# A fused attention and mixture-of-experts layer on one core: the key's rotation sum and the application of both layer norms, moved between VectorE and GpSimd

## The reference

```
xn  = (x - mean) / sqrt(var + 1e-5)                       # first layer norm
q   = rope(rms_norm(xn @ wq));  k = rope(rms_norm(xn @ wk));  v = xn @ wv      # 16 / 4 / 4 heads of 128
kc  = rms_norm(ctx @ wk_ctx);   vc = ctx @ wv_ctx
x1  = x + softmax(q @ [kc k]^T / sqrt(128) + causal) @ [vc v] @ wo
xn2 = (x1 - mean) / sqrt(var + 1e-5)                      # second layer norm
out = x1 + shared_ffn(xn2) + sum over the top 2 of 8 experts of weight * expert_ffn(xn2)
rope(k) = k * cos + rotate_half(k) * sin
```

## Time and profile before

| | |
|---|---|
| median of 3 runs | 366.74 us (364.2, 366.74, 368.2) |
| the profiled execution's own time | 366.01 us |
| its span | 364.3 us |
| mean granted clock of TensorE | 0.989 of full speed |
| instructions | 7426 |
| busy share of the span | PE 91%, PEld 61%, DVE 87%, ACT 72%, POOL 46% |

### The profile page before, as it was taken

One profiled execution on the slowest core, in us unless ns is written; L12 is line 12 of the kernel. 1 busy time (PEld: TensorE's weight loads), 2 busy tenths in 40 slices (PEclk: granted clock), 3 DMA queues, 4 the chain that ended last, 5 costly groups with the idle time before them and its releaser, 6 DMA issues.

```text
span 364.3 us, 7426 instructions
## 1 busy us (share of the span) xinstructions
PE 329.9 (91%) x2296; PEld 223.4 (61%) x2296; DVE 316.9 (87%) x602; ACT 263.7 (72%) x916; POOL 166.5 (46%) x241
## 2 busy tenths in 40 slices
PE   6788698799999999999999999999999999987894
PEld 6365455376667666866576657565856687754351
DVE  1779999998999899989999998999899987967643
ACT  3668989576986798679768976897599748447341
POOL 4467656652755175427532734263426230362600
PEclk9899989999999999999999999999999999999999
DMA  6977000000042005200300000000000000167844
GB/s 177 380 238 230 18 0 2 1 2 14 1 126 47 14 0 128 45 14 3 58 6 8 0 0 14 0 0 0 0 0 0 3 0 0 23 123 75 159 75 129
DMA packets 34835, 19.25 MB, mean 53 GB/s; under 512 B 24056, under 2 KB 32256, under 8 KB 34816
## 3 DMA queue, kind: packets, MB, share of 16 engines
q1 hardware_dynamic: 34816, 19.02, 20.6%
HBM read 12.20 MB, written 1.05 MB: 36 GB/s over the span
## 4 chain that ended last, share of the span: by engine, by line
PE 35%; DVE 24%; ACT 18%; issue 10%; POOL 6%; DMA 3%; SPq 1%; DVEq 1%; ACTq 0%; POOLq 0%
PE proj L1352 10%; ACT probs L549 7%; DVE probs L982 5%; PE pt_ps L1315 5%; PE turn L1261 3%; DVE nmax L970 3%; POOL q_rot L772 3%; PE o_ps L1325 3%; DVE pT_lo L908 3%; PE proj L1172 3%; PE sc_ps L1282 3%; ACT pT_hi L460 2%; DVE q_t L899 2%; ACT kc_junk L493 2%; DMA wq<-in_L_xattn_wq_dram 2%
## 5 line engine op out<-in xcount | busy, mean ns | idle before, releaser
L549 ACT ACTIVATE probs<-sc_ps,nbias,q_r 128x256 f32<-128x256 f32 x128 | 70.8, 573 | 2.8 <-DVE nbias L974 2.8
L772 POOL TENSOR_TENSOR q_rot<-q_t 128x512 f32<-128x512 f32 x32 | 42.4, 1325 | 41.3 <-DVE q_t L901 40.5
L982 DVE TENSOR_SCALAR probs<-probs,rden 128x256 f32<-128x256 f32 x128 | 51.2, 461 | 1.1
L460 ACT ACTIVATE pT_hi<-pt_ps 128x512 f16<-128x512 f32 x64 | 34.8, 597 | 10.1 <-PE pt_ps L1315 10.1
L493 ACT ACTIVATE q_junk<-proj 128x128 bf16<-128x128 f32 x128 | 34.0, 294 | 10.8 <-DVE q_t L901 10.8
L1172 PE MATMUL proj<-wq_hi,xT 128*128 128x512 f16 x128 | 39.2, 389 | 2.1 <-DVE wq_lo L892 2.1
L908 DVE SCALAR_TENSOR_TENSOR pT_lo<-pt_ps,pT_hi 128x512 f16<-128x512 f32 x64 | 40.9, 680 | 0.1
L970 DVE TENSOR_REDUCE nmax<-sc_ps 128x4 f32<-128x1024 f32 x32 | 38.8, 1214 | 1.5 <-PE sc_ps L1304 1.5
L729 POOL TENSOR_TENSOR q_r<-q_me,power 128x4 f32<-128x4 f32 x32 | 33.4, 1044 | 2.5
L460 ACT ACTIVATE qT_hi<-turn 128x512 f16<-128x512 f32 x32 | 19.5, 610 | 20.5 <-PE turn L1261 20.5
L1315 PE MATMUL pt_ps<-ident,probs 128*128 128x128 f32 x256 | 34.1, 277 | 0.2
(11 more groups left out here) (221 smaller groups left out, 882.8 us busy)
## 6 DMA issues: line engine op xcount, KB each, us to landing
wq<-in_L_xattn_wq_dram SPq DMA_DIRECT2D x4, 512.0 KB, 8.4
w<-in_L_ffn_w_dram SPq DMA_DIRECT2D x2, 1024.0 KB, 9.9
wq<-in_L_xattn_wo_dram SPq DMA_DIRECT2D x1, 2048.0 KB, 8.2
ctx_b<-in_ctx_dram SPq DMA_DIRECT2D x8, 128.0 KB, 2.0
out_dram<-x_all SPq DMA_DIRECT2D x4, 256.0 KB, 2.2
x_all<-in_x_dram SPq DMA_DIRECT2D x1, 896.0 KB, 12.0
wkc<-in_L_xattn_wk_ctx_dram SPq DMA_DIRECT2D x1, 512.0 KB, 3.9
wk<-in_L_xattn_wk_dram SPq DMA_DIRECT2D x1, 512.0 KB, 4.9
```

The lines of the kernel that those rows point to most:

```text
L460: return nc.scalar.activation(out_, in_, ACT.Copy, scale=scale)
L549: last = nc.scalar.activation(probs[:, h, :], sc_ps[:, h, :], ACT.Exp, bias=nbias[:, h:h + 1], scale=q_r[:, g, h:h + 1], accum_out=den[:, ...
L772: nc.gpsimd.tensor_tensor(q_rot[:], q_t1[:], q_t2[:], ALU.add).then_inc(q_added, 1)
L982: last = nc.vector.tensor_scalar(probs[:, h, :], probs[:, h, :], rden[:, h:h + 1], None, ALU.mult)
```

## The change

Three steps of rows change engine. `k_add` for the key of the next row goes from the end of DVE's g = 2 to POOL's g = 2, between `q_add` and `k_roots`. `ln_scale` for the next row goes from DVE's g = 1 to POOL's g = 0, right behind `ln_root`. `second_norm` for the row before goes from DVE's g = 2 to POOL's g = 1, right behind `l2_root`. In the prologue DVE still does `k_add(0)` and `ln_scale(0)`, and behind the rows it still does `second_norm(7)`; so each of the three moves in 7 of its 8 executions. DVE gains two waits in `scores_max` (for the first norm's application at g = 0, for the second's at g = 1), one in its own `second_norm` and one ahead of the last residual; they keep it from overwriting statistics that POOL still reads. On POOL the loop over rows 4 to 6 is written out.

```diff
--- before.py
+++ after.py
@@ -734,6 +734,12 @@
                 pool.wait_ge(ln_root1, nb + 1)
                 nc.gpsimd.tensor_tensor(ln_rs[:], ln_r1[:], scale_x[:], ALU.mult).then_inc(ln_rstd, 1)
 
+            def ln_scale(nb):
+                pool.wait_ge(ln_rstd, nb + 1)
+                seen(pool, ln_lo, nb)
+                nc.gpsimd.tensor_scalar(xs[:], x_all[:, nb, :], ln_mv[:, 0:1], ln_rs[:, 0:1],
+                                        ALU.subtract, ALU.mult).then_inc(ln_xs, 1)
+
             def ln_low(nb):
                 pool.wait_ge(ln_hi, nb + 1)
                 seen(pool, in_turned, nb)
@@ -743,6 +749,11 @@
                 seen(pool, l2_done, b)
                 rstd(ln2_mv, ln2_ve, ln2_rs, l2_aggr, l2_var, l2_rstd, b + 1)
 
+            def second_norm(b):
+                pool.wait_ge(l2_rstd, b + 1)
+                nc.gpsimd.tensor_scalar(xn2_all[:, b, :], x_all[:, b, :], ln2_mv[:, 0:1], ln2_rs[:, 0:1],
+                                        ALU.subtract, ALU.mult).then_inc(l2_done, 1)
+
             def kc_roots(nb):
                 seen(pool, kc_norm, nb)
                 inv_rms(kc_ss[:], kc_me[:], kc_r[:], eps_kc, kc_sq, kc_mean, kc_root, nb + 1)
@@ -750,6 +761,11 @@
             def k_roots(nb):
                 seen(pool, k_norm, nb)
                 inv_rms(k_ss[:], k_me[:], k_r[:], eps_k, k_sq, k_mean, k_root, nb + 1)
+
+            def k_add(nb):
+                pool.wait_ge(k_t12, nb + 1)
+                seen(pool, k_norm, nb)
+                nc.gpsimd.tensor_tensor(k_sum[:], k_t1[:], k_t2[:], ALU.add).then_inc(k_added, 1)
 
             def k_scale(nb):
                 pool.wait_ge(k_added, nb + 1)
@@ -800,6 +816,7 @@
                         q_add(*ahead_of(b, g, 2, last))
                     if g == 0 and first:
                         ln_root(b + 1)
+                        ln_scale(b + 1)
                     if g == 2 and not last:
                         kc_roots(b + 1)
                     if ahead_of(b, g, 2, last):
@@ -809,9 +826,12 @@
                             q_roots(*ahead_of(b, g, 2, last))
                     if g == 0 and not first and not last:
                         ln_root(b + 1)
+                        ln_scale(b + 1)
                     if g == 1 and not first:
                         l2_root(b - 1)
+                        second_norm(b - 1)
                     if g == 2 and not last:
+                        k_add(b + 1)
                         k_roots(b + 1)
                         k_scale(b + 1)
                         q_roots(b + 1, 0)
@@ -845,7 +865,7 @@
             row(1, False, False, cast_to(w1_b, w1_32, d_w1, w1_cast))
             row(2, False, False, cast_to(w3_b, w1_32, d_w3, w3_cast))
             row(3, False, False, cast_to(w2_b, w2_32, d_w2, w2_cast))
-            with pool.Fori(4, B - 1) as b:
+            for b in range(4, B - 1):
                 row(b, False, False)
             row(B - 1, False, True)
 
@@ -967,6 +987,10 @@
             def scores_max(b, g):
                 u = G * b + g
                 dve.wait_ge(s_done, u + 1)
+                if g == 0:
+                    dve.wait_ge(ln_xs, b + 1)
+                if g == 1:
+                    seen(dve, l2_done, b - 1)
                 nc.vector.tensor_reduce(nmax[:], sc_ps[:], AX_X, ALU.max, negate=True).then_inc(s_max, 1)
                 dve.wait_ge(s_max, u + 1)
                 dve.wait_ge(q_root, u + 1)
@@ -1000,6 +1024,7 @@
 
             def second_norm(b):
                 dve.wait_ge(l2_rstd, b + 1)
+                seen(dve, l2_done, b)
                 nc.vector.tensor_scalar(xn2_all[:, b, :], x_all[:, b, :], ln2_mv[:, 0:1], ln2_rs[:, 0:1],
                                         ALU.subtract, ALU.mult).then_inc(l2_done, 1)
 
@@ -1032,8 +1057,6 @@
             def row(b, first, last):
                 for g in range(G):
                     u = G * b + g
-                    if g == 1 and first:
-                        ln_scale(b + 1)
                     scores_max(b, g)
                     if g == 3 and first:
                         wo_split(0)
@@ -1041,12 +1064,8 @@
                         split_low(wv32[:], wv_hi[:], wv_lo[:], G + 2)
                     if ahead_of(b, g, 1, last):
                         q_low(*ahead_of(b, g, 1, last))
-                    if g == 1 and not first and not last:
-                        ln_scale(b + 1)
                     if g or not first:
                         p_low(u - 1)
-                    if g == 2 and not first:
-                        second_norm(b - 1)
                     if ahead_of(b, g, 2, last):
                         q_turn(*ahead_of(b, g, 2, last))
                     if g == 0 and not last:
@@ -1074,8 +1093,6 @@
                         v_low(b)
                     if g or not first:
                         o_low(u - 1, (g - 1) % G)
-                    if g == 2 and not last:
-                        k_add(b + 1)
                     if g == 0:
                         vc_low(b)
 
@@ -1139,6 +1156,7 @@
             o_low(G * B - 1, G - 1)
             e_scale(0)
             e_scale(1)
+            dve.wait_ge(l2_done, B - 1)
             residual(B - 1)
             e_scale(2)
             second_norm(B - 1)
```

## The result

The changed kernel takes **368.80 us** (median of 20 runs, 365.74 to 370.41) beside 366.48 us for the kernel before (20 runs): a ratio of **1.0057 [1.0034, 1.0081]**, or about 2.1 us. The forecast was 367.0 us and no measurable change: the range held, and the change is a little slower, by less than 1%. Its working did not hold everywhere. The six steady rows were forecast at +0.9 us and give +0.3; row 0 was forecast at -0.5 us and gives +1.3 in the profiled execution and, to judge by their longer times, more in most others.

The account below looks back on a forecast made before the run. PE, ACT and POOL in turn bound the steady rows, DVE in g = 0 alone. Rows 1 to 6 +0.9 and row 0 -0.5 gave +0.4: 366.4 us profiled, 367.1 against the median, stated 367.0; range 364.2 to 369.5 us.

Parts of the forecast that it names:

- the two terms of the sum: Whole kernel: rows 1 to 6 together +0.9 us and row 0 -0.5 us, giving +0.4 us.
- What bounds the kernel: Steady rows: PE last in g = 1, ACT, POOL, PE in g = 2, ACT in g = 3, DVE in g = 0 alone.
- DVE's busy time "about 13 us lower": Sign expected in the changed profile: DVE's busy time about 13 us lower, its waits for ACT in g = 3 longer.
- Rows 1 to 6, +0.15 us each: Steady rows: -0.06 second norm, +0.16 key's sum, +0.05 DVE's new waits; six rows make +0.9 us.
- the +0.16: POOL in g = 2, rows 1 to 6: the key's sum at 1.27 us starts the root 0.16 us late, whole into the row.
- The new wait at g = 0: DVE's added wait ahead of nmax in rows 1 to 6: 0 to +0.10 us per row, taken as +0.05.
- the second norm's gain: DVE in g = 2, rows 1 to 6: an earlier reciprocal lets POOL's first root come earlier, 0 to -0.06 us, taken as -0.06.
- The norms on POOL: POOL in g = 0 and g = 1: 0.67 us each, priced from x_lo, hidden in POOL's waits for ACT.
- Row 0, -0.5 us: Row 0: part of DVE's freed time counts and moves wo_lo forward; bounds -0.93 and 0 us, taken as -0.5.
- DVE as the bound: Rival, rows' DVE work: if all counted, 13.4 us gained and 353.4 us; only the key's sum, 359.0 us. Chance 0.11.
- The second: Rival, g = 2: a DVE instruction holds up POOL's key sum to 2.25 us; +6.8 us, 373.5 us. Chance 0.09.
- What the prediction held more likely there: g = 2 of steady rows: by the exclusive lock, k_add would hold up DVE's bias rather than be held.

Follow-up runs that it names:

- 3: 40 small TensorE products put in row 1's wait before the mix: changed kernel 366.96 us, ratio 1.0002; kernel before 366.09 us, 0.9992.
- 4: Changed kernel with DVE's second split of wo in row 0 in four pieces: 368.93 us, 1.0079; with 40 small TensorE products as well 367.31 us, 1.0009.
- 2: POOL's wo_lo in eight pieces: changed kernel 364.07 us, ratio 0.9930; kernel before 365.15 us, 0.9953.
- 6: POOL's scaling of wo and wo_lo each in eight pieces: changed kernel 364.41 us, ratio 0.9933; kernel before 364.13 us, 0.9926.

## Why the prediction was right, and where it was wrong

- **The range held, with some luck.** The time is 1.8 us above the forecast, and the two terms of the sum were off in opposite directions.
- **What bounds the kernel: right.** DVE lost 6.3 us of busy time and none of rows 1 to 6 got shorter. After the sum's place it waits for ACT in g = 2 and g = 3, as argued.
- **DVE's busy time "about 13 us lower": wrong, 6.3.** By groups, 13.4 us left DVE and the bias's group grew from 8.9 to 11.1 us, so the groups' sum fell by 10.9 (340.7 to 329.8). Records of neighbours overlap at their ends, the page counts the overlap once, and there was 4.6 us more of it before: I had read 13 us of groups as 13 us of engine.
- **Rows 1 to 6, +0.15 us each: right in sign, mis-sized.** Measured +0.04 between the two profiled executions, which is hardly more than their scatter: over all executions here the six rows take 213.12 to 213.29 us with the steps moved and 212.99 to 213.24 without. The key's sum cost 1.27 us as taken from q_rot, and k_me starts at its end. But of the +0.16 only +0.08 arrives: from ACT's squares of the context key (kc_junk) to the last reciprocal it is 10.07 us instead of 9.99. The new wait at g = 0 showed nothing, where 0.05 was taken; the second norm's gain, taken as -0.06, is -0.03 at POOL's q_rot (2.65 us behind the first of ACT's squares, not 2.68).
- **The norms on POOL: mis-sized, 1.23 us against 0.67.** The nearest row was of another kind (two tensors, rounded to f16). In rows 1 to 7 POOL's waits hide them. In row 0 ACT's x_hi waits 0.54 us for it.
- **Row 0, -0.5 us: this step failed.** The gain on DVE was there (0.75 us up to row 1's first maximum). What was wrong is "wo_lo starts behind DVE's rotation, so what DVE gains moves wo_lo forward too". wo_lo starts behind POOL's root, which waits for ACT's squares, and these came only 0.40 us earlier (q_me at +34.53, not at +34.93). DVE's split, 0.75 us earlier, then met the root. I wrote that k_r would meet DVE's split and gave that no price; k_r took 1.02 us there, 1.01 before. It was q_r, and in the profiled execution it cost 1.1 us on POOL and 1.0 us of hold. Nor has the sum a term for TensorE's clock behind the wait, and that is where the loss lies: with the clock kept (3) it is gone. That the met root and the longer hold bring the clock down is not shown: in 4 both were nearly undone and the loss stayed. With DVE's split in pieces and the 40 products together, the forecast's size is there, in one execution: the hold is 2.19 us, the clock 1.00, and `out_proj` of row 1 comes 48.89 us behind row 0's first maximum, against 49.45 before: -0.56.
- **The rivals.** DVE as the bound did not come true. The second had the right mechanism, a DVE instruction that makes POOL wait, in the wrong place: in g = 2 of the steady rows k_sum took 1.27 to 1.29 us. What the prediction held more likely there came: in row 4 the bias took 0.35 us instead of 0.16 and ended with k_sum (203.34 + 0.35 = 203.69 against 202.39 + 1.29 = 203.68).

What stays open: how the moves in row 0 make the clock fall more often or for longer, and why executions of one kernel differ. What a longer hold costs by itself is open too: with the clock kept it was 0.54 us in one pair of executions, and cutting it from 3.39 to 2.19 us gave nothing in the medians. Cutting it from 2.18 to 0.67 us gave 0.47% in the kernel before, but the clock, which falls in some runs of that kernel as well, may be part of this.

## What to carry to other kernels

Work moved off an engine that isn't the bound is worth nothing, but it shifts which instructions of two engines run side by side; look in the startup stage for long ones that could swap places, not only in the steady loop. A long GpSimd instruction beside VectorE's short ones on the path was better issued in pieces: it took 1 us more in itself here and gave 0.5 to 0.7%. When a stage is slower than its parts explain, read TensorE's granted clock in the stretch behind the longest wait, in more than one execution: one profile of each kernel gave a wrong idea here of which of them loses the clock.

## What the runs showed of the hardware

- The Trainium skill (SBUF — State Buffer, § Who interferes with whom) says that the order of issue, not the shape, decides who blocks. These traces agree in both directions: the same bias of 128x4 waited 3.17 us for POOL's wo_lo, and POOL's root, 1.01 us alone, took 2.10 behind a VectorE split that began with it. A root that is first did not hold the split, though: before, the split began 0.31 us into the root (63.37 against 63.06) and took its usual 1.22 us.
- A wait of TensorE of one length had different ends: behind 2.52 us the kernel before kept a granted clock of 1.00, and the changed kernel undone in row 0 fell to 0.85 (68 to 72 us) and 0.72 (72 to 76 us); with DVE's split in pieces it fell to 0.67 behind 2.72 us, and behind 3.74 us 72 to 76 us ran at 0.50. Behind waits of about 1 us and less (2 and 6) every profiled execution kept 1.00.
- The norm, one tensor and two scalars per partition, takes GpSimd as long on 128x256 (1.23 us) as the sum of two tensors on 128x512 (1.27 us); VectorE took 0.40.
